# x loaded transposed and scaled on GpSimd, k's maxima subtracted inside ScalarE's exp, in a fused attention layer on Trainium2

## The reference

```python
xn = ln(x) * ln_w + ln_b
q = softmax(xn @ Wq + bq, over the 32 channels of a head)
k = softmax(xn @ Wk + bk + (1 - mask) * -1e6, over the 64 positions)
v = (xn @ Wv + bv) * mask
att = einsum('bnhd,bnhl->bhdl', k, v);  y = einsum('bnhd,bhdl->bnhl', q, att)
scale, shift = split(silu(cond) @ W_emb + b_emb)          # per sequence
out = x + silu(ln2(y) * (1 + scale) + shift) @ W_out + b_out
```

## Time and profile before

| | us |
|---|---|
| median of 3 runs | 323.29 (321.79 to 323.85) |
| profiled execution, its own time | 323.25 |
| its span, first to last instruction | 321.4 |
| PE busy | 308.0 (96% of the span) |
| DVE busy | 275.1 (86%) |
| POOL busy | 229.4 (71%) |
| ACT busy | 193.0 (60%) |

### The profile page before, as it was taken

One profiled execution on the slowest core, in us unless ns is written; L12 is line 12 of the kernel. 1 busy time (PEld: TensorE's weight loads), 2 busy tenths in 40 slices (PEclk: granted clock), 3 DMA queues, 4 the chain that ended last, 5 costly groups with the idle time before them and its releaser, 6 DMA issues.

```text
span 321.4 us, 14568 instructions
## 1 busy us (share of the span) xinstructions
PE 308.0 (96%) x5664; PEld 263.4 (82%) x5664; DVE 275.1 (86%) x749; ACT 193.0 (60%) x378; POOL 229.4 (71%) x276
## 2 busy tenths in 40 slices
PE   7899989999999999999999999999999999999974
PEld 6577867887988898988888898988889898988864
DVE  3775989889797998989898989989898989988883
ACT  1449384667486575668485675757575765756360
POOL 2170459778778687878887787878788887889550
PEclk9999999999999999999999999999999999999979
DMA  7930301050412204040403214050403110010023
GB/s 213 353 110 0 100 4 37 2 167 4 130 38 72 92 8 155 2 163 0 131 32 97 66 42 121 0 163 0 145 19 119 44 65 0 12 55 2 4 68 131
DMA packets 21706, 23.84 MB, mean 74 GB/s; under 512 B 1073, under 2 KB 19121, under 8 KB 21682
## 3 DMA queue, kind: packets, MB, share of 16 engines
q1 hardware_dynamic: 20192, 21.89, 22.0%
q10 hardware_dynamic: 1490, 1.62, 1.5%
HBM read 15.12 MB, written 8.39 MB: 73 GB/s over the span
## 4 chain that ended last, share of the span: by engine, by line
PE 82%; DVE 7%; DMA 4%; issue 2%; ACT 1%; POOL 1%; SPq 1%; POOLq 1%; DVEq 0%
PE bv L890 27%; PE bk L890 27%; PE by L890 13%; PE by L966 4%; PE by L945 4%; PE bv L957 4%; PE by L1026 4%; DMA x_all<-in_x 4%; DVE ystat L769 1%; DVE xstat L621 1%; DVE y_s L760 1%; DVE xt_lo L789 1%; DVE k_t L800 1%; ACT xhat L550 1%; POOLq L45 1%
## 5 line engine op out<-in xcount | busy, mean ns | idle before, releaser
L349 POOL TENSOR_TENSOR k_t<-k_t,kmax 128x512 f32<-128x512 f32 x32 | 34.4, 1074 | 26.3 <-DVE kmax L804 26.3
L496 ACT ACTIVATE k_t<-k_t 128x512 f32<-128x512 f32 x32 | 20.0, 626 | 44.5 <-POOL k_t L349 44.5
L267 POOL TENSOR_TENSOR z_s<-z_s,mod_shift 128x512 f32<-128x512 f32 x30 | 30.7, 1043 | 14.2 <-DVE z_s L720 14.2
L360 POOL TENSOR_TENSOR h_lo<-h_s,h_hi 128x512 fp32r<-128x512 f32 x30 | 38.5, 1306 | 2.9 <-ACT h_hi L513 2.3
L368 POOL TENSOR_TENSOR x_all<-x_all,bo_all 128x1024 f32 (+1 forms) x16 | 38.9, 2434 | 0.0
L550 ACT ACTIVATE xhat<-x_all,xr 128x256 f32 (+1 forms) x62 | 32.2, 591 | 4.6 <-DVE xr L632 3.1
L416 POOL TENSOR_SCALAR y_s<-y_s,yr 128x256 f32<-128x256 f32 x60 | 32.7, 558 | 2.5 <-POOL yr L413 2.2
L800 DVE SCALAR_TENSOR_TENSOR k_t<-off,bk 128x512 f32<-128x512 f32 x32 | 21.9, 683 | 14.5 <-PE bk L890 14.5
L890 PE MATMUL bv<-w_o_hi,h_hi 128*128 128x256 f32 x120 | 32.3, 288 | 0.0
L890 PE MATMUL bv<-w_o_lo,h_hi 128*128 128x256 f32 x120 | 32.2, 290 | 0.0
L520 ACT ACTIVATE xt_hi<-by 128x512 fp32r<-128x512 f32 x32 | 17.4, 597 | 23.4 <-PE by L1026 23.4
(11 more groups left out here) (128 smaller groups left out, 867.2 us busy)
## 6 DMA issues: line engine op xcount, KB each, us to landing
x_all<-in_x SPq DMA_DIRECT2D x15, 512.0 KB, 4.6
out<-x_all SPq DMA_DIRECT2D x15, 512.0 KB, 3.2
off<-in_mask_rows SPq DMA_DIRECT2D x16, 256.0 KB, 3.3
x_all<-in_x SPq DMA_DIRECT2D x2, 256.0 KB, 3.7
z_s<-in_w_emb ACTq DMA_DIRECT2D x1, 512.0 KB, 9.7
h_s<-in_w_emb ACTq DMA_DIRECT2D x1, 512.0 KB, 12.3
out<-x_all SPq DMA_DIRECT2D x2, 256.0 KB, 2.6
y_s<-in_wk ACTq DMA_DIRECT2D x1, 256.0 KB, 3.8
```

What stands on the lines that cost most here:

```text
L267: return eng.tensor_tensor(z, z, mod_shift[:, c, span(g, GB)].unsqueeze(2).broadcast_to([P, GB, SEQ]), ALU.add)
L349: nc.gpsimd.tensor_tensor(kk, kk, kmax[:, c, :].unsqueeze(2).broadcast_to([P, GB, SEQ]), ALU.subtract).then_inc(ksub_d, 1)
L360: nc.gpsimd.tensor_tensor(h_lo[:, c, :], h_s[:, c, :], h_hi[:, c, :].bitcast(fp32), ALU.subtract).then_inc(hlo_d, 1)
L496: nc.scalar.activation(k_t[:, parity, c, :], k_t[:, parity, c, :], ACT.Exp).then_inc(kexp_d, 1)
```

## The change

- A second input `x_t` holds x transposed (256 x 8192). SP loads 512 columns of it per group into `xt_raw` (double buffered, `load_xt`).
- POOL scales it: times a row of reciprocal deviations, plus a row of offsets (`x_scaled`, four 128x512 operations per group), in place of xhat and PE's x transposes. Only group 0 keeps the old way.
- These rows hold one value per position, the same in all partitions. POOL computes them as before, one per partition (`x_rstd`), DVE transposes them in 32x32 blocks (`x_rows`), SP stores them to DRAM in four DMAs of 128-byte pieces (`rows_stored`) and loads them back to all 128 partitions, 4 KB each (`rows_loaded`, one buffer).
- ACT's xt_hi and DVE's xt_lo read `xt_raw` in SBUF and stand at the end of turn i-1.
- k: DVE writes mask*1e6 - k and takes the minimum; ACT's exp subtracts with scale -1 and kmax as bias, eight activations of 128x64 per half. POOL's subtraction is gone.
- y's scaling goes from POOL to ACT (`y_hat_all`), but for group 14.
- x is loaded three groups ahead, its statistics are taken three groups ahead (S marks that group i+3 exists), in turn 0 those of groups 1, 2 and 3.
- Orders: on DVE kmax of half 1 behind z_scaled, x_stats between the two h_products, q's maxima ahead of y_sums and its subtraction behind; on ACT q_exp of tiles 2, 3 between the two copies of e_k and that of tiles 0, 1 at the end of the turn before; on POOL x_scaled of half 0, h_low twice, x_scaled of half 1. Turns 13 and 14 are outside of the loop.

```diff
+            def load_xt(g, parity):
+                sp.dma_start(xt_raw[:, parity, :, :], xt_h[:, :, span(g, GT)]).then_inc(xt_in[parity], 16)
+
+            def rows_stored(g, parity):
+
+                wait(sp, xrow_d, g)
+                wait(sp, rows_in, 16 * g - 32)
+                for n in range(4):
+                    sp.dma_start(rows_dram[parity].rearrange("k (t p) -> (k t) p", p=P)[:, 32 * n:32 * n + 32],
+                                 xr_rows[32 * n:32 * n + 2 * T, :]).then_inc(rows_out, 16)
+
+            def rows_loaded(g, parity):
+
+                wait(sp, rows_out, 64 * g)
+                wait(sp, xs_d, 2 * g - 2)
+                sp.dma_start(rows[:, :, :].rearrange("p k n -> p (k n)").unsqueeze(1),
+                             rows_dram[parity:parity + 1].rearrange("o k n -> o (k n)").unsqueeze(0)
+                             .broadcast_to([P, 1, 2 * GT])).then_inc(rows_in, 16)
...
+            def body(i, par, N, F, B, O, S):
+
+                if S:
+                    if not (isinstance(i, int) and i < 0):
+                        wait(sp, xstat_d, 4 * i + 5)
+                    load_x(i + 3, 1 - par)
                 if N and not (isinstance(i, int) and i < 1):
-                    wait(sp, xstat_d, 4 * i)
-                    load_x(i + 1, 1 - par)
                     wait(sp, kadd_d, 2 * i)
                     load_off(i + 1, 1 - par)
+                if not (isinstance(i, int) and i + 2 >= G):
+                    rows_stored(i + 2, par)
                 if O and not (isinstance(i, int) and i < 3):
                     store(i - 3)
+                if not (isinstance(i, int) and i + 2 >= G):
+                    if not (isinstance(i, int) and i < 0):
+                        if not first(i):
+                            wait(sp, lo_d, 2 * i + 2)
+                        load_xt(i + 2, par)
+                    rows_loaded(i + 2, par)
...
-            def k_shifted(g, parity, c):
-
-                wait(pool, kmax_d, 2 * g + c + 1)
-                kk = k_t[:, parity, c, :].rearrange("p (b s) -> p b s", s=SEQ)
-                nc.gpsimd.tensor_tensor(kk, kk, kmax[:, c, :].unsqueeze(2).broadcast_to([P, GB, SEQ]),
-                                        ALU.subtract).then_inc(ksub_d, 1)
...
+            def x_scaled(g, parity, c):
+
+                if c == 0:
+                    wait(pool, rows_in, 16 * g)
+                    wait(pool, xt_in[parity], 8 * (g + parity))
+                xc = xt_raw[:, parity, c, :]
+                nc.gpsimd.tensor_tensor(xc, xc, rows[:, 0, :], ALU.mult).then_inc(xm_d, 1)
+                wait(pool, xm_d, 2 * g + c - 1)
+                nc.gpsimd.tensor_tensor(xc, xc, rows[:, 1, :], ALU.add).then_inc(xs_d, 1)
...
+                for c in range(C):
+                    if N and c == 0:
+                        x_scaled(i + 1, 1 - par, c)
+                    if O:
                         h_low(i - 2, c)
-                if F and not last_turn(i):
...
+            def x_high(g, parity, c):
+
+                wait(act, xs_d, 2 * g + c - 1)
+                wait(act, qv_d, 4 * g)
+                nc.scalar.activation(xt_hi[:, c, :], xt_raw[:, parity, c, :], ACT.Copy).then_inc(hi_d, 1)
...
             def k_exp(g, parity, c):
-                wait(act, ksub_d, 2 * g + c + 1)
-                nc.scalar.activation(k_t[:, parity, c, :], k_t[:, parity, c, :], ACT.Exp).then_inc(kexp_d, 1)
+
+                wait(act, kmax_d, 2 * g + c + 1)
+                for n in range(GB):
+                    kk = k_t[:, parity, c, n * SEQ:n * SEQ + SEQ]
+                    last = nc.scalar.activation(kk, kk, ACT.Exp, scale=-1.0, bias=kmax[:, c, n:n + 1])
+                last.then_inc(kexp_d, 1)
...
+                    exp_k_copied(i - 1, 0)
+                    q_exp(i - 1, 1 - par, 1)
+                    exp_k_copied(i - 1, 1)
...
+                v_tile(i, par, 0)
                 if O:
+                    h_high(i - 2, 0)
+                v_tile(i, par, 1)
+                if O:
+                    h_high(i - 2, 1)
+                k_exp(i, par, 1)
+                v_tile(i, par, 2)
+                v_tile(i, par, 3)
+                if N:
+                    mask_offset(i + 1, 1 - par)
                     for c in range(C):
-                        h_high(i - 2, c)
-                if N:
-                    g = i + 1
-                    wait(act, xr_d, 4 * g + 4)
-                    wait(act, xt_d, 2 * g - 2)
-                    for t in range(T) if not (isinstance(g, int) and g == 0) else (0, 1):
-                        nc.scalar.activation(xhat[:, 1 - par, t, :],
-                                             group_of(x_all, g)[:, :, t * D:t * D + D].rearrange("p g n -> p (g n)"),
-                                             ACT.Identity, scale=xr[:, 1, t:t + 1],
-                                             bias=xr[:, 3, t:t + 1]).then_inc(xhat_d, 1)
-                if F:
-                    if last_turn(i):
-                        k_exp(i, par, 1)
-                    v_tile(i, par, 2)
-                    v_tile(i, par, 3)
-                    if not last_turn(i):
-                        k_exp(i, par, 1)
-                if N and not (isinstance(i, int) and i < 0):
-                    mask_offset(i + 1, 1 - par)
+                        x_high(i + 1, 1 - par, c)
+                q_exp(i, par, 0)
...
+            def x_rows(g):
+
+                wait(dve, xr_d, 4 * g + 4)
+                wait(dve, rows_out, 64 * g - 64)
+                nc.vector.transpose(xr_rows[:, :], xr[:, :, :].rearrange("p a t -> p (a t)")).then_inc(xrow_d, 1)
...
+            def x_low(i, c, full):
+
+                wait(dve, hi_d, 2 * i + c + 1)
+                nc.vector.tensor_tensor(xt_lo[:, c, :], full, xt_hi[:, c, :].bitcast(fp32),
+                                        ALU.subtract).then_inc(lo_d, 1)
...
+                if first(i):
                     for c in range(C):
-                        wait(dve, hi_d, 2 * i + c + 1)
-                        nc.vector.tensor_tensor(xt_lo[:, c, :], bt[c][:, :], xt_hi[:, c, :].bitcast(fp32),
-                                                ALU.subtract).then_inc(lo_d, 1)
-                if isinstance(i, int) and i == 0:
+                        x_low(0, c, bt[c][:, :])
                     silu_cond()
                     x_stats(1, 1)
-                for c in range(C):
-                    if F:
-                        wait(dve, k_d, 2 * i + c + 1)
-                        wait(dve, off_d, i + 1)
-                        if c == 0:
-                            wait(dve, ekt_d, 2 * i - 2)
-                        nc.vector.scalar_tensor_tensor(k_t[:, par, c, :], off[:, par, :], -1000000.0, bk_[c][:, :],
-                                                       ALU.mult, ALU.add).then_inc(kadd_d, 1)
-                        wait(dve, kadd_d, 2 * i + c + 1)
-                        wait(dve, ksub_d, 2 * i + c - 1)
-                        nc.vector.tensor_reduce(out=kmax[:, c, :],
-                                                in_=k_t[:, par, c, :].rearrange("p (b s) -> p b s", s=SEQ),
-                                                axis=AX.X, op=ALU.max).then_inc(kmax_d, 1)
+                k_masked(i, par, 0)
+                k_max(i, par, 0)
+                k_masked(i, par, 1)
                 if O:
                     z_scaled(i - 2)
+                k_max(i, par, 1)
                 if isinstance(i, int) and i == 1:
                     modulation()
-                if N and not (isinstance(i, int) and i == 0):
-                    x_stats(i + 1, 1 - par)
-                if isinstance(i, int) and i == 0:
+                if first(i):
+                    x_rows(1)
                     weights_qv()
+                    x_stats(2, 0)
                 if B:
                     kv_scaled(i - 1)
+                if not (isinstance(i, int) and i + 2 >= G) and not first(i):
+                    x_rows(i + 2)
                 if O:
                     h_product(i - 2, 0)
+                if S:
+                    x_stats(i + 3, 1 - par)
+                if O:
                     h_product(i - 2, 1)
                 if isinstance(i, int) and i == 1:
                     weights_o()
-                if F:
-                    q_tiles(i, par, (0, 1))
+                q_max(i, (0, 1))
                 if B:
                     y_sums(i - 1)
+                q_shifted(i, par, (0, 1))
+                if B:
                     y_scaled(i - 1, 0)
                     y_scaled(i - 1, 1)
                     y_stats(i - 1, (0, 1, 2, 3))
-                if F:
-                    q_tiles(i, par, (2, 3))
+                q_max(i, (2, 3))
+                q_shifted(i, par, (2, 3))
+                if first(i):
+                    x_rows(2)
+                if N:
+                    for c in range(C):
+                        x_low(i + 1, c, xt_raw[:, 1 - par, c, :])
...
-                        if c == 0:
```

(4 more changed lines are left out.)

## The result

The kernel after takes 332.31 us (median of 4 runs, 331.18 to 333.07), the kernel before 323.24 us beside it: a ratio of 1.0268, 95% interval 1.0221 to 1.0315. It is slower. The profiled execution's span is 329.4 us against 321.4. What came out is rival B's price of a steady group (18.25 us), not the forecast's; B's 335 us is 2.7 too high.

What follows compares the result with a forecast made beforehand. The prediction took PE to bound the kernel before at 17.87 us per group, DVE close behind. Span 321.4 + 5.9 (start) - 10.0 (steady groups) + 1.0 (tail) = 318.3, plus 1.85 outside: 320.2 us; range 315 to 332.

Steps and rivals of the forecast that it cites:

- rival B: Steady groups: POOL's multiply starts before h_s every time, DVE bounds at 18.25 us per group, 335 us; chance 0.25 with half way.
- PE: Groups 1 to 15 lose their x transposes, 11.3 us on the chain; PE's limit becomes 17.0 us per group.
- ACT: Sixteen small exps replace two: 14.1 us per group, bounds 11.8 to 16.4, under 17.0 in any case.
- POOL: Subtractions and y scalings go, four x operations come: 14.5 to 16.1 us per group, under 17.0.
- The lock: DVE's h_s against POOL's large operations: h_s first, second h_s waits 0.5 us, 17.1 us per group, bounds 17.0 to 18.3.
- the sums put it 0.1 us ahead: Argument for POOL's multiply starting before h_s: estimated starts of 4.9 against 5.0 us in a group.
- two semaphores: Argument for h_s first: POOL's multiply must wait for the rows and transposed x, h_s for nothing more.
- POOL pays 0.7: If h_s starts first, POOL's x multiply loses 0.7 us to it in each group.
- The rows' way: Start: SP's queue delays x(3) and x(4), x_stats waits; losses of 3.5 and 2.2 us, 5.9 in all at group 2.
- the longer landing: Row stores at the start: 128-byte pieces argued for slower landing, taken as 2.5 us.
- The tail: Last group: q's exp between e_k's copies delays attention by 1.0 us, bounds 0 and 1.3.
- The sum: Whole span: 321.4 + 5.9 - 10.0 + 1.0 = 318.3 us; with 1.85 outside, 320.2 us.

Runs made afterwards that it cites:

- tie_tiny: tie with POOL's two x scaling operations of the second half cut from 512 to 4 columns, that half left mostly unscaled: 316.39 us (0.9799).
- one_exp: Kernel after with one 128x512 exp per half of k instead of eight of 128x64, using the first sequence's maximum for all: 329.72 us (1.0222).
- tie: Kernel after with one more wait: POOL's first multiply of the transposed x begins only when the first h_s is done: 330.77 us (1.0192).
- tiny_x0: Kernel after with POOL's two scaling operations of the first half of transposed x cut from 512 to 4 columns: 318.86 us (0.9885).
- tiny_x1: Kernel after with POOL's two scaling operations of the second half of transposed x cut from 512 to 4 columns: 328.63 us (1.0178).
- tail_only: Kernel after with only the tail's order restored, both copies of e_k ahead of q's second exp: 330.41 us (1.0244).
- x_early: Kernel after with the loads of x(3) and x(4) ahead of the row stores and loads in SP's queue: 331.23 us (1.0277).
- before_kexp: Kernel before with k negated, its maxima subtracted in sixteen 128x64 exps and POOL's two k subtractions gone: 326.2 us (1.0085).
- late_bias: rstd_gap with one more wait: POOL's addition of b_out to x begins only when both xt_lo of the next group are done: 345.81 us (1.0731).
- refill: Kernel after with POOL's work reordered (first-half x operations one group earlier, b_out addition before yr), h_s paired, x loads and tail copies earlier: 344.01 us (1.0698).
- rstd_gap: Kernel after with both h_s back to back, both h_low before the x operations, POOL's small xr operations moved behind the shifts: 362.79 us (1.1197).

## Why the prediction was wrong

**PE**: right. 17.00 us in tie_tiny. In the kernel after only the last two groups, 17.04 and 17.12 us, come near it.

**ACT**: eight exps take 2.02 us (1.8 taken), 335 ns each. ACT 14.44 us (14.1). The Trainium skill ("ScalarE: Activation LUTs", What ACT_TABLE_LOAD costs) gives 0.28 us plus 0.83 ns an element for an activation with a pointer bias, 0.333 us here; the trace agrees. "Under 17.0 in any case" held, and one_exp shows that the exps don't set the 18.2 us. But it asks too little: once h_s is free, as in tie, ACT's 2.0 us stand in a round through ACT, DVE and POOL.

**POOL**: 15.92 us (14.5 to 16.1), by x operations of 1.29 us, not 1.02. The shifts' second operand is one value per 64 columns, the rows a full 128x512 tensor; h_lo, with two full tensors, had 1.27 per operation in the earlier trace rows and was the row to take. No run changes the operand alone, so the reason is argued from these rows. The Trainium skill ("GPSIMD Engine Reference", Elementwise — side-by-side cycle accounting) gives some 2.6 cycles an element for two inputs, 1.11 us here by estimate; the trace has more.

**The lock**: the step that failed, at the choice that h_s is first. POOL's multiply was first by 0.33 to 0.6 us in every steady group; "the sums put it 0.1 us ahead" was in the text, and was set aside for two semaphores; the multiply follows the shifts with no idle time, so neither held it. The two h_s cost 2 x 1.376 - 1.31 = 1.44 us more (rival B: 1.65), the groups take 18.2 (18.25). tiny_x0 and tiny_x1 show that this is the cause: the cut beside h_s gives 0.97 us back per group, the same cut elsewhere nothing. B's 335 is too high mostly because its 13 x 0.38 = 4.9 us came out as -0.35 (start and tail, 1.45 us dearer than in its sum, take a part of that back): the last two groups, without x_stats, come down to 17.1 us, 2.3 less together, and the stretch that it counts takes 234.45 us in the kernel before, 2.1 more than 13 x 17.87 (its first three groups take 18.9, 18.7 and 18.2). The forecast's -10.0 leaves out the same 2.1.
The second error is worth as much: had h_s won, 17.1 us would still have been wrong. tie shows 17.95. A group lasts as long as the longest round of dependences through the engines, which can be more than the largest sum over one of them, and no round was added up. The prediction had one price of it, "POOL pays 0.7" if h_s is first, and left it out of the sum; in tie's round POOL pays 1.0.

**The rows' way**: the two waits are there, at 25 and 40 us, 3.65 and 1.79 us long (5 and 2 said, for losses of 3.5 and 2.2). The stores were cheaper (0.33 us each to issue, not 0.48, and the rows' load could be issued 0.9 us after the fourth, not 2.5: the longer landing that was argued for isn't there), the load of x dearer (5.3 and 6.4 us to landing). Of the 7.05 us at group 2, 1.7 vary from run to run: in tail_only, with the same code up to there, xt_lo of group 2 ends at 52.35, +5.3. The 5.9 said lie between, and that is partly luck. In tail_only xt_lo of group 1 is 1.4 us later than before, not 3.5, and the next group loses 3.9, not 2.4: 1.9 by the wait and 1.7 because the two operations on w_o, beside POOL's x operations, take 1.21 and 1.38 us instead of 0.42 and 0.43, the lock once more, at a place that the prediction didn't count. In x_early both waits go and the loss stays (+6.4 at group 2, 1.1 more than in tail_only, which starts alike), so the mechanism as told, SP's queue alone, wasn't enough: the time then goes to DVE's wait for POOL's xr and to its operations beside POOL's large ones.

**The tail**: +1.3 (1.0 said), but the copies' order, to which it was put down, is worth 0.25; before_kexp, with the old order, has +1.5. The traces point at the lock again: the last group's h_s (both in the kernel after, the second in before_kexp) stand beside POOL's addition of b_out (294.01 to 296.41 us in the kernel after), which starts there since the k subtraction is gone, and counted from xt_lo they end 1.0 us later than before (1.4 in before_kexp). No run moved that addition alone, so the sixteen exps aren't ruled out.

**The sum**: 5.9 - 10.0 + 1.0 = -3.1 was forecast, 7.05 - 0.35 + 1.3 = +8.0 came. 9.65 of the 11.1 us between them are those of the 13 groups.

## What to carry to other kernels

Work moved to POOL has two prices: its own duration, taken from a row with the same kinds of operands, and what stands beside it. List DVE's operations with two inputs in SBUF (here two pairs, h_s and xt_lo) and see what POOL does at those times, before and after. An order that works may do so because small operations stand there, and moving them moves the collision. Ask also who pays when the other engine comes second, and whether a round goes through it.
A tie of 0.1 us in a sum of estimated starts is a coin, and a forecast that rests on one should stand between its sides.
When an engine's sum is close to the limit, add up the round of dependences too (from an operation to its own next turn): here it held 18.0 us with no engine busier than 17.5 (PE in tie; DVE 16.6).

## What was not expected

A DVE operation on 128x4 numbers took 0.86 to 1.03 us in late_bias and up to 1.81 in refill instead of 0.17, when a large POOL operation was running (the first on yr): this tensor_scalar from SBUF to SBUF waited as h_s does, with one SBUF input. Likewise at the start of the kernel after the cast of w_o took 1.38 us, 0.43 before.
TensorE's lower clock made a 2.3 us wait cost 4.4 us (rstd_gap). The kernel after itself, with 0.7 us of gaps in a group, kept 1.00 throughout its steady groups.
The first xt_lo started at 10.5 to 11.4 us in most traces and at 13.5 to 13.9 in five of them, that of the kernel after among them. What decides it stays open, as does whether some order with all the work done reaches 17.0 us.
